# Two expert networks of a hybrid block: output products with stationary weights in two 64-column tiles

## What is computed

```python
# L2 ffn: 8 experts, hidden 256, top 2 of 8
top_w, top_i = top_k(xf @ Wg + bg, 2);  top_w = softmax(top_w)
for e in range(8):
    h = gelu(xf @ W1[e] + b1[e])
    out = out + w_dense[:, e:e+1] * (h @ W2[e] + b2[e])
# L3 attn: windowed mean, gated by sigmoid(tanh(x Wp + bp) Wg), window of 16 tokens
# L3 ffn: 16 experts, hidden 128, top 2 of 16
hidden = silu(x @ w1[e]) * (x @ w2[e])
out = sum over e of (hidden @ w3[e]) * dispatch[:, e]
```

## Time and profile before

| | |
|---|---|
| median of 3 runs | 553.65 us (549.29 to 553.72) |
| the profiled execution | 553.72 us, of which the span of the trace is 551.9 us |
| mean granted TensorE clock | 0.944 of full |
| first network, from its first hidden matmul to the first of the second | 313.1 to 410.2 us |
| second network, to the end of its last output matmul | 410.2 to 543.9 us |
| what follows to the last store | 8 us |

### The profile page before, as it was taken

One profiled execution on the slowest core, in us unless ns is written; L12 is line 12 of the kernel. 1 busy time (PEld: TensorE's weight loads), 2 busy tenths in 40 slices (PEclk: granted clock), 3 DMA queues, 4 the chain that ended last, 5 costly groups with the idle time before them and its releaser, 6 DMA issues.

```text
span 551.9 us, 9422 instructions
## 1 busy us (share of the span) xinstructions
PE 485.1 (88%) x3372; PEld 412.7 (75%) x3372; DVE 369.8 (67%) x1052; ACT 267.9 (49%) x629; POOL 163.8 (30%) x175
## 2 busy tenths in 40 slices
PE   0989999978718699869999999999999989999994
PEld 0677666643417599769999899899999969879793
DVE  2299477417875857895878744455577896786754
ACT  1484555542306578756889744444453322223230
POOL 4800000000230517270223432231353434353331
PEclk9996999997957889997999999999999988999998
DMA  8300000000030203000000000000000000000000
GB/s 158 122 2 1 1 1 1 1 0 2 0 76 2 67 11 79 1 0 2 1 2 2 2 1 1 1 1 1 2 0 1 1 1 2 1 5 15 2 10 11
DMA packets 5458, 8.14 MB, mean 15 GB/s; under 512 B 2850, under 2 KB 4514, under 8 KB 4900
## 3 DMA queue, kind: packets, MB, share of 16 engines
q1 hardware_dynamic: 5268, 7.43, 5.8%
q10 hardware_dynamic: 144, 0.11, 0.1%
HBM read 7.01 MB, written 0.52 MB: 14 GB/s over the span
## 4 chain that ended last, share of the span: by engine, by line
PE 67%; DVE 23%; issue 4%; ACT 3%; DMA 1%; POOL 0%; SPq 0%; DVEq 0%; ACTq 0%; POOLq 0%
PE PS L1632 10%; PE PS L1600 9%; PE PS L1617 9%; PE PS L1362 7%; PE PS L1346 7%; PE PS L1581 6%; PE PS L1505 3%; PE PS L1517 3%; PE PS L1307 2%; DVE M L917 2%; DVE Y L973 2%; DVE QL L1002 2%; PE PS L1446 2%; DVE Y L975 2%; ACT score_arena L711 1%
## 5 line engine op out<-in xcount | busy, mean ns | idle before, releaser
L510 POOL TENSOR_TENSOR pr<-pr 128x512 f32<-128x512 f32 (+2 forms) x70 | 67.2, 960 | 129.3 <-DVE pr L1015 56.1
L743 ACT ACTIVATE VV<-PS 128x512 f32<-128x512 f32 x64 | 38.2, 597 | 90.7 <-PE PS L1632 90.7
L1617 PEld LDWEIGHTS PS<-wk,hid 128*128 128x128 f32 x512 | 68.7, 196 | 5.9
L1600 PEld LDWEIGHTS PS<-wk,hid 128*128 128x128 f32 x512 | 66.6, 191 | 6.4 <-ACT hid L733 1.2
L711 ACT ACTIVATE score_arena<-score_arena,nmx 128x128 f32<-128x128 f32 (+1 forms) x128 | 56.9, 447 | 22.8 <-DVE nmx L1110 22.2
L733 ACT ACTIVATE hid<-PS,wk 128x512 f32<-128x512 f32 x64 | 43.8, 687 | 49.2 <-PE PS L1581 49.2
L1617 PE MATMUL PS<-wk,hid 128*128 128x64 f32 x512 | 65.7, 272 | 0.0
L1600 PE MATMUL PS<-wk,hid 128*128 128x64 f32 x512 | 63.9, 268 | 0.7 <-ACT hid L733 0.7
L1241 DVE TENSOR_TENSOR hid<-VV,PS 128x512 f32<-128x512 f32 x64 | 43.8, 685 | 26.7 <-PE PS L1632 17.6
L1632 PE MATMUL PS<-YTs,WH 128*128 128x512 f32 x128 | 58.7, 458 | 2.1 <-DVE hid L1241 2.1
L654 ACT ACTIVATE st_mem<-PS 128x512 f32<-128x512 f32 x72 | 39.3, 595 | 35.7 <-PE PS L1362 35.7
(11 more groups left out here) (223 smaller groups left out, 1057.8 us busy)
## 6 DMA issues: line engine op xcount, KB each, us to landing
stage<-in_wexp SPq DMA_DIRECT2D x6, 512.0 KB, 5.9
wk<-in_w SPq DMA_DIRECT2D x1, 1032.0 KB, 8.9
wa<-in_wat SPq DMA_DIRECT2D x1, 768.0 KB, 7.2
cst<-in_consts SPq DMA_DIRECT2D x1, 580.0 KB, 8.1
X<-in_x SPq DMA_DIRECT2D x2, 256.0 KB, 6.2
out<-X SPq DMA_DIRECT2D x16, 32.0 KB, 1.9
wc<-in_w SPq DMA_DIRECT2D x2, 183.5 KB, 7.4
score_arena<-in_wcv SPq DMA_DIRECT2D x2, 144.0 KB, 7.8
```

The lines of the kernel that those rows point to most:

```text
L510: step(nc.gpsimd.tensor_tensor(buf[:, :, 0:width], buf[:, :, 0:width], buf[:, :, width:2 * width], ALU.add))
L1600: ins = mm(accumulator(u, q, e % UNIT), hid[:, v % 3, q * P:(q + 1) * P], wk[:, W128["w2_2"]][:, r * C:(r + 1) * C], start=False, stop=(v ...
L1617: ins = mm(accumulator(u, q, e % UNIT), hid[:, v % 3, q * P:(q + 1) * P], wk[:, W128["w3"]][:, e * C:(e + 1) * C], start=True, stop=True)
```

## The change

It rewrites the output products of both networks, and what stands around them.

- **Output products.** The weights (`W2`, `w3`, 128 rows by 64 columns) become the stationary operand and `hid` moves, 512 tokens at a time. The result is channel-major, 64 rows. Two experts (a pair) are done together: one writes PSUM partitions 0 to 63, the other 64 to 127, of one bank. The first network has 16 units (4 pairs by 4 chunks) with two halves each, so 32 groups of two such products; the second has 32 units with one group each.
- **Gates.** They must now vary along the free axis. `split_gate` (VectorE) puts a high and a low fp32r part of a chunk's gates into `gate_parts`; fills tB and tD transpose it; ScalarE copies it to `gate_rows`; for each unit one 512-column fp32r matmul with the constant `pick` spreads two experts' gates over the 128 partitions (`spread_gate`), and ScalarE copies that to `gate_wide`.
- **Sum.** `combine` is one VectorE operation for a unit: (bank + `b2`) x `gate_wide`, or bank x `gate_wide`, into `weighted` or, for a chunk's first pair, `acc`. GpSimd adds `weighted` to `acc` (128x512). At a chunk's end fill fC or fE (`token_sum`) multiplies `acc` with the constant `halves`, four products of 64 columns, which adds the two halves and goes back to token-major; `take_sum` on VectorE adds it to `T`.
- **Buffers.** Four hidden banks (0, 1, 2, 6) and four `hid` slots in place of three; bank 6 was the attention's.
- **Layer norm inside the networks.** `ln_out` and `ln_evac` are spread: GpSimd scales (`ln_scale`), ScalarE makes the high part (`y_high`) and copies the transposes (`y_evac`), VectorE keeps the low part (`ln_low`).
- **Gone:** the bias matmuls, the row of `b2`, its transfer and its split on GpSimd.

```diff
-FIRST_FILLS = {12: ("yB", 3), 14: ("gB", 3), 27: ("yC", 0), ...
+FIRST_FILLS = {0: (("tB", 0),), 5: (("yB", 3),), 6: (("gB", 3), ("tB", 1)), 10: (("fC", 0),), 13: (("yC", 0),), ...
+HID_BANKS = (0, 1, 2, 6)
+GATE_BANK = 5
...
+            def ln_scale(c):
+                ln_power(c)
+                pool.wait_ge(lninv_ready, norms[0])
+                ts = slice(4 * c, 4 * c + 4)
+                nc.gpsimd.tensor_tensor(Y[:, ts], Y[:, ts], lnst[:, 2, ts].unsqueeze(2).to_broadcast([P, CHUNK, C]), ALU.mult).then_inc(yn_ready, 1)
...
+            def add_unit(u):
+                c, p = divmod(u, PAIRS2) if u < UNITS2 else divmod(u - UNITS2, PAIRS3)
+                if p == 0:
+                    return
+                pool.wait_ge(combined, u + 1)
+                nc.gpsimd.tensor_tensor(acc[:, c % 2], acc[:, c % 2], weighted[:, u % 2], ALU.add).then_inc(acc_added, 1)
...
+            def copy_gate(u):
+                act.wait_ge(gate_spread, u + 1)
+                if u >= 2:
+                    act.wait_ge(combined, u - 1)
+                nc.scalar.activation(gate_wide[:, u % 2], PS[:, GATE_BANK, :], ACT.Copy).then_inc(gate_copied, 1)
+            for n in range(4 * UNITS2):
...
+                if i == 3:
+                    copy_gate(u)
+                if n in (1, 13, 29, 43, 63):
+                    copy_rows(*{1: ("tB", 0), 13: ("tB", 1), 29: ("tB", 2), 43: ("tB", 3), 63: ("tD", 0)}[n])
+                if n in (6, 23, 39, 47, 63):
+                    y_high({6: 3, 23: 0, 39: 0, 47: 1, 63: 1}[n])
+                if n in (11, 27, 43, 49):
+                    y_evac(*{11: ("yB", 3), 27: ("yC", 0), 43: ("yD", 0), 49: ("yC", 1)}[n])
...
-                for i in range(2):
-                    nc.vector.tensor_tensor(pr8[...], PS[:, 3 + 2 * (u % 2) + i, :]..., gate[...], ALU.mult).then_inc(acc_free, 1)
+                if u < UNITS2:
+                    nc.vector.scalar_tensor_tensor(to, PS[:, 3 + u % 2, :], wk[:, W128["b2"]][:, p:p + 1], gate_wide[:, u % 2],
+                                                   ALU.add, ALU.mult).then_inc(combined, 1)
+                else:
+                    nc.vector.tensor_tensor(to, PS[:, 3 + u % 2, :], gate_wide[:, u % 2], ALU.mult).then_inc(combined, 1)
...
+            def first_out(q):
+                u, ht = divmod(q, 2)
+                if ht == 0 and u >= 2:
+                    pe.wait_ge(combined, u - 1)
+                pe.wait_ge(gelu_done, 2 * q + 2)
+                for i in range(2):
+                    r = tile2(u, 2 * ht + i)
+                    ins = mm(PS[i * C:(i + 1) * C, 3 + u % 2, :], wk[:, W128["w2_2"]][:, r * C:(r + 1) * C],
+                             hid[:, (2 * q + i) % 4], start=(ht == 0), stop=(ht == 1))
+                ins.then_inc(out2_done, 1)
+            def second_out(r):
+                u = UNITS2 + r
+                pe.wait_ge(combined, u - 1)
+                pe.wait_ge(prod3_done, 2 * r + 2)
+                for i in range(2):
+                    e = 2 * (r % PAIRS3) + i
+                    ins = mm(PS[i * C:(i + 1) * C, 3 + u % 2, :], wk[:, W128["w3"]][:, e * C:(e + 1) * C],
+                             hid[:, (2 * r + i) % 4], start=True, stop=True)
+                ins.then_inc(out3_done, 1)
...
-                    for q in range(CHUNK):
-                        ins = mm(accumulator(u, q, e % UNIT), hid[:, v % 3, q * P:(q + 1) * P],
-                                 wk[:, W128["w2_2"]][:, r * C:(r + 1) * C], start=False, stop=(v % (2 * UNIT) == 2 * UNIT - 1), skip_group_check=True)
```

More of the change, by code:

```diff
@@ new lines, in gate_logits @@
+            def gate_logits(name, c, bias, E):
+                take_logits(name, c, bias, E)
+                top_first(name, c, E)
+            for u in range(UNITS2):
+                combine(u)
+                if u == 0:
+                    ln_low(3)
+                if u == 1:
+                    split_gate(0, 1)
+                if u == 2:
+                    gate_logits("gB", 3, rw[:, ROWS["bg2"]], E2)
+                if u == 3:
+                    top_second(E2)
+                if u == 4:
+                    take_sum("fC", 0)
+                    ln_stats(0)
+                    top_gate(3, E2)
+                if u == 5:
+                    ln_low(0)
+                    split_gate(0, 2)
+                if u == 6:
+                    window_bias(0)
+                if u == 7:
+                    window_logits(0)
+                    window_gate(0)
+                if u == 8:
+                    window_add(0)
+                    ln_stats(0)
+                    take_sum("fC", 1)
+                if u == 9:
+                    split_gate(0, 3)
+                    ln_low(0)
+                    ln_stats(1)
+                if u == 10:
+                    ln_low(1)
+                if u == 11:
+                    gate_logits("gD", 0, rw[:, ROWS["bg3"]], E3)
+                if u == 12:
+                    window_bias(1)
+                    top_second(E3)
+                if u == 13:
+                    window_logits(1)
+                    top_gate(0, E3)
+                    split_gate(1, 0)
+                    window_gate(1)
+                    take_sum("fC", 2)
+                if u == 14:
+                    window_add(1)
+                    ln_stats(1)
+                if u == 15:
+                    ln_low(1)
+                    ln_stats(2)
@@ new lines, in _ @@
+                if r == 18:
+                    take_sum("fE", 1)
+                if r == 19:
+                    take_logits("gD", 3, rw[:, ROWS["bg3"]], E3)
+                    output(1)
+                if r == 20:
+                    top_first("gD", 3, E3)
+                if r == 21:
+                    top_second(E3)
+                if r == 22:
+                    top_gate(3, E3)
+                    split_gate(1, 3)
+                if r == 26:
+                    take_sum("fE", 2)
@@ L1290, in _ @@
+                if r == 27:
+                    output(2)
+            combine(UNITS2 + UNITS3 - 1)
+            take_sum("fE", 3)
             output(3)
@@ new lines, in gate_turn @@
+            def gate_turn(name, c):
+                pe.wait_ge(parts_ready, 4 * (name == "tD") + c + 1)
+                take(name, c)
+                for q in range(CHUNK):
+                    ins = nc.tensor.transpose(PS[:, 7, q * P:(q + 1) * P], gate_parts[:, q, :], ident)
+                ins.then_inc(misc_filled, 1)
+            def first_out(q):
[8 more added lines that the diff above has]
+                ins.then_inc(out2_done, 1)
@@ L1621, in _ @@
[L1621 to L1627 removed]
+                if ht == 1:
+                    spread_gate(u)
+                if q >= 1:
+                    first_out(q - 1)
+                for what in FIRST_FILLS.get(q, ()):
+                    more(what)
```

481 lines of the change are left out of this document (259 added, 222 removed).

## The result

The changed kernel takes 580.34 us (median of 4 runs, 577.6 to 581.3) against 553.41 us of the kernel before on the same chip: a ratio of 1.0496, 95% interval 1.0435 to 1.0557. It is 26.9 us slower, where 20.7 us faster was forecast; the miss is 47.3 us. The profiled execution has a span of 578.1 us.

The account below looks back on a forecast made before the run. TensorE was taken to bound both networks. Loops -18.2 and -14.7, bias matmuls -3.7, gate transposes +2.8, token sums +5.7, waits +5 and +2.4 gave -20.7 us: 553.7 to 533.0, range 516 to 547 (8 in 10).

Parts of the forecast that it names:

- Output products: Both networks: two products side by side in the array's column halves cost 1.02 us a pair; bounds 0.86 and 1.78.
- The halves one after the other: Rival for the output products: the two halves do not work side by side, 1.78 us; about 582 us, chance 0.05.
- a drain of the size of that rival: Rival: every change of tile shape drains the array, up to 20 us over 64 groups; about 553 us, chance 0.07.
- Steady cost of the loops: Loops of both networks: 2.15 and 3.18 us per pair, 68.8 and 101.8 us, saving 18.2 and 14.7 us.
- Waits in the first network: First network: TensorE waits behind ScalarE's in-order queue and late norm and gate inputs; +5 us, bounds 0 and 12.
- behind Gelu 6: First network: the high part of chunk 3's norm waits in ScalarE's queue, so TensorE stands some 3 us.
- the four slots hide most of it: First network: the norm chain returns for chunks 0 and 1, mostly hidden by four slots; +1 us.
- Waits in the second network: Second network: VectorE's load against TensorE's, 0.87, and clumped top-2 choices; 13 us booked, +2.4, bounds 4 and 24.
- the old kernel's 10.6 us: Second network before the change: 133.7 us less TensorE's 123.1, time counted as lost, the base for the 13 us.
- not a bound: Second network: GpSimd's 28 additions at 1.28 us make 36 us, where its folds took 44, so GpSimd does not bound.
- The slow clock: After a TensorE wait the clock was granted at 0.50, so matmuls take twice as long; more such stretches possible, unpriced.
- given back in waits: Rival: waits of both networks at their upper bounds, 18 us above the forecast's; about 551 us, chance 0.12.

Follow-up runs that it names:

- loops alone: Kernel before and changed kernel, each with the small steps between and inside the two networks' expert loops left out: 540.3 and 510.1 us.
- re-placed kernel: Changed kernel with the same instructions, but side work of TensorE, VectorE, ScalarE and GpSimd set at other loop steps: 533.5 us, ratio 0.9668.

## Why the prediction was wrong

- **Output products: right.** 1.02 us a pair forecast, 1.01 measured, from the earlier trace rows. The halves one after the other are out, and so is a drain of the size of that rival (20 us); of a change of tile shape 0.10 us more than forecast shows, in the matmul ahead of each group. The price for two products is that of one. The Trainium skill's page "TensorEngine Tiling (Array Packing)" gives up to twice the speed for such a dimension (section Overview); here it is 1.62 / 1.01 = 1.6 times.
- **Steady cost of the loops: 8.4 us too low.** 68.8 and 101.8 us forecast, 73.8 and 105.2 measured (first hidden matmul to the end of the loops alone). The matmul ahead of a change of tile shape costs 0.33 in place of 0.23 us, once for each of the 64 groups, which is 6.4 us. The earlier trace rows could not show it, because the output product there does not change the tile shape: the matmul ahead of it costs 0.23 and only the one behind it 0.32. Another 1.4 us is the wait for the first gate rows, which the prediction had among the waits.
- **Waits in the first network: the step that failed, by 11 us.** "Total +5 us; bounds 0 and 12." The network is 26.0 us longer than its loops alone (clock included), where the forecast had 15.2. The waits named are there: TensorE stood 1.25 us behind Gelu 6, where 3 were forecast, and 1.36 for the first gate rows, where 1 was. But the list was made of three kinds of place, and the trace has ten waits of 0.7 us and more, eight of them ahead of fills: for the window's result, for a bank that VectorE had not freed, for rows not yet copied. "Where the four slots hide most of it" was never worked out: four slots hide a lateness in the loop, and none at a fill, which TensorE's queue reaches in its turn.
- **Waits in the second network: the step that failed, by 27.5 us.** "I book 13 us, +2.4; bounds 4 (-7) and 24 (+13)." The network is 51.7 us longer than its loops alone, forecast 24.2. VectorE's busy time was forecast well (97.8 us; 106.0 with 13 us of hold-ups), but the waits were scaled from a ratio of busy times, 0.87 against 0.83, and put down to VectorE's products, for which TensorE waited 1.5 us in all. The re-placed kernel shows what the ratio is worth: with 103.6 us of VectorE against 118.2 of TensorE, 0.88, it stands still for 7.9 us. Waits came from where each step stands in its queue, and a ratio doesn't know that. The prediction kept the old kernel's 10.6 us as a base, although the change set every place in every queue anew, for a loop faster by a tenth.
- **GpSimd: "not a bound" is true, and the wrong question.** It was busy for 48.4 of 157.3 us, and its additions cost 24.7 us, 17.5 of them because they read SBUF beside VectorE.
- **The slow clock** stood in a rival, as a reason to raise it, and had no price. It came to 17.1 us, over a third of the miss. The sign that the prediction set for it, below 0.9 in either network, was just not met (0.97 and 0.90), and its other two signs of being wrong (a group over 1.3 us, ScalarE busy for nearly all of the first network) were not met either: none looked at TensorE's standing still.
- **The rival "given back in waits"** had the mechanism, with 551 us and 0.12. Its size was capped by the bounds of the two wait terms, which had been chosen around the estimate and not worked out from what happens when fills are late and the clock falls. With 30 us of standing and 17 of clock on top, as measured, it would have ended on the slower side.
- **The forecast of 533.0 us** is what the re-placed kernel takes (533.5; networks 84.1 and 126.1, forecast 84 and 126). In part that is luck: loops 8.4 us longer, side work 8.2 us cheaper than the forecast.

## What to carry to other kernels

When a change makes the bounding loop faster, the work placed between its steps by hand must be costed as a schedule: for each fill, when its input is ready and when the queue gets there, with every hand-over. Busy shares and their ratios said nothing on it here. Put nothing into an in-order queue before its input is there, since what it holds is the loop, or the copy that the next fill needs. A long operation of an engine off the path may still hold another: look for small operations that last a microsecond. And before the time between two traces is given to an edit, compare the stretches that the edit did not touch: the clock can differ there.

## What was not expected of the hardware

- One fp32 product with 64 stationary columns, on half of the array between full-width matmuls, costs 1.00 us, and two, one on each half, 1.01. The full-width matmul ahead of them costs 0.33 us in place of 0.23.
- A GpSimd addition of two SBUF operands makes a VectorE operation on 128x4 last 1.05 us instead of 0.16; a GpSimd fill of the same length leaves it at 0.16, but holds a copy (1.04).
- Behind a wait of TensorE of 5.2 us the granted clock averaged 0.66 over the next 7.9 us; with unused matmuls in the wait it stayed at 1.00. Elsewhere the same instructions with the same waits ran at 0.69 in one trace (16.5 us) and at 1.00 in two others (12.1 us).
